# The third feed-forward part of a decoder: token lists per expert in place of all experts for every token

## The reference, cut to what matters

```python
shared = gelu(x @ ws1 + bs1) @ ws2 + bs2
aff = softmax(x @ Wr + br)                 # 31 experts
vals, idx = top_k(aff, 3)
gates = sum(one_hot(idx, 31) * vals[..., None], axis=-2)
for e in range(31):
    routed += gates[..., e] * (gelu(x @ We1[e] + Be1[e]) @ We2[e] + Be2[e])
x = layernorm(x + shared + routed + x)     # the part's own "+ x" and the residual
```

## Time and profile before

| | us |
|---|---|
| median of 3 runs (lowest, highest) | 2757.01 (2756.97, 2764.75) |
| the profiled execution, its own time | 2757.16 |
| its span, first to last instruction | 2755.4 |
| mean granted clock of TensorE | 0.846 |

### The profile page before, as it was taken

How to read it: one execution, slowest core, us unless ns; L and a number is a source line. 1 busy time by engine, 2 the same in 40 slices (tenths; PEclk the granted TensorE clock), 3 DMA queues, 4 the chain that set the end, 5 groups by cost and what they waited for, 6 DMA issues and landing times. The chain is left out here.

```text
span 2755.4 us, 44085 instructions
## 1 busy us (share of the span) xinstructions
PE 2173.7 (79%) x15402; PEld 1094.6 (40%) x15402; DVE 1629.0 (59%) x3578; ACT 1194.6 (43%) x2185; POOL 654.1 (24%) x845
## 2 busy tenths in 40 slices
PE   2699999975899996658999988629687773768888
PEld 1133355433233342634554444228422221335556
DVE  4588766577777732455676545235567772436666
ACT  0277756642267753223666675304232211433332
POOL 4211111134201110432121112044236673100000
PEclk9699999976589997777999998659888875779998
DMA  3300011100101010521111000038400001111111
GB/s 116 114 25 25 27 36 38 29 15 23 35 25 27 17 27 1 172 89 50 35 30 37 20 20 17 12 102 298 149 0 1 0 1 25 30 47 54 54 62 47
DMA packets 106846, 133.01 MB, mean 48 GB/s; under 512 B 26006, under 2 KB 90326, under 8 KB 105987
## 3 DMA queue, kind: packets, MB, share of 16 engines
q1 hardware_dynamic: 101556, 115.32, 14.0%
q0 software_dynamic: 3776, 7.79, 0.8%
q10 hardware_dynamic: 1296, 7.08, 0.7%
HBM read 70.65 MB, written 13.49 MB: 31 GB/s over the span
## 5 line engine op out<-in xcount | busy, mean ns | idle before, releaser
L1326 ACT ACTIVATE probs<-psE 128x512 f32<-128x512 f32 (+2 forms) x1248 | 698.0, 584 | 405.7 <-PE psE L1165 229.4
L1450 DVE TENSOR_REDUCE maxima<-psM 128x2 f32<-128x1024 f32 (+4 forms) x640 | 678.9, 1082 | 312.7 <-PE psM L1142 142.7
L1165 PE MATMUL psE<-q_stack,k_stack 53*128 53x512 bf16 (+3 forms) x1152 | 372.1, 361 | 36.6 <-ACT probs L1326 26.3
L1142 PE MATMUL psM<-k_stack,q_stack 51*128 51x512 bf16 (+3 forms) x1280 | 358.9, 352 | 32.2 <-DVE maxima L1450 13.9
L1601 POOL TENSOR_SCALAR pool_t<-mean_var 128x4 f32<-128x4 f32 x60 | 15.0, 250 | 935.7 <-DVE mean_var L1387 931.0
L2299 DVE SCALAR_TENSOR_TENSOR hres<-psM,gates,hres 128x128 f32<-128x128 f32 x512 | 144.2, 345 | 81.8 <-PE psM L2233 81.0
L1165 PEld LDWEIGHTS psE<-q_stack,k_stack 53*128 53x128 bf16 x1152 | 98.2, 94 | 229.2 <-ACT probs L1326 144.8
L1142 PEld LDWEIGHTS psM<-k_stack,q_stack 51*128 51x128 bf16 x1280 | 101.5, 96 | 196.2 <-issue 105.6
L1077 PE MATMUL psM<-masks_bf,ident_bf 64*128 64x128 bf16 (+2 forms) x832 | 148.3, 260 | 16.7 <-DMA k_stack<-k_parts 15.8
L2233 PEld LDWEIGHTS psM<-values,probs 128*128 128x128 f32 x1024 | 136.5, 195 | 59.4 <-issue 58.9
L1185 PE MATMUL psB<-probs,values 128*32 128x256 f32 (+3 forms) x1712 | 154.3, 432 | 2.4 <-ACT probs L1326 1.0
(11 more groups left out here) (411 smaller groups left out, 3614.4 us busy)
## 6 DMA issues: line engine op xcount, KB each, us to landing
q_stack<-q_parts SPq DMA_DIRECT2D x432, 64.0 KB
values<-experts_dram SPq DMA_DIRECT2D x40, 514.0 KB, 4.7
values<-experts_dram SPq DMA_DIRECT2D x32, 512.0 KB, 3.2
k_stack<-k_parts SPq DMA_DIRECT2D x192, 64.0 KB
hid<-experts_dram SPq DMA_DIRECT2D x15, 514.0 KB, 4.4
work<-experts_dram SPq DMA_DIRECT2D x15, 514.0 KB, 4.7
pack<-pack_dram SPq DMA_DIRECT2D x1, 4647.0 KB
work<-sorted SPq DMA_DIRECT2D x70, 65.0 KB, 3.7
```

The source lines that it names most:

```text
L1142: out, len(heads), keys, lo, max_mask(c, t), lambda i, to, start, stop: nc.tensor.matmul(to, q_stack[lo:lo + R_MAX, job.a % Q_SLOTS, pair_ ...
L1165: lambda h, to, start, stop: nc.tensor.matmul(to, ks[lo:lo + R_END, pairs[h], k * P:k * P + c.kn], q_stack[lo:lo + R_END, job.a % Q_SLOTS, ...
L1326: nc.scalar.activation(probs[0:c.kn, m % 2, heads[0]:heads[-1] + 1, q0:S], psE[0:c.kn, n % 2, 0:len(heads) * (S - q0)].rearrange("p (h q) ...
L1450: nc.vector.tensor_reduce(top, psM[:, at:at + len(banks), 0:per * keys].rearrange("p b (h k) -> p b h k", h=per), AX_X, ALU.max, negate=Tr ...
```

## The change

Part 3 now runs in `routed_experts` with n_exp = 31, top = 3, one block of 128 hidden features (`ft=1`), gelu in place of relu, and `shared=True`. `moe_stage`, `route` and `choose` are gone. NT is 16 * 3 + 30 = 78 tiles. The shared expert is computed for all tokens ahead of the tile loop: four up products of 512 tokens, four gelus, and its down product added in the bank of the experts' second biases. The output is stored from SP.

```diff
-        moe_stage(3, E3, E3 - 1, K3, 1, ACT.Gelu, "experts3", 4, residuals=2,
-                  store=lambda u: io["out"].rearrange("b (t p) d -> p b t d", p=P)[:, u:u + 1])
+        routed_experts(3, E3 - 1, K3, "experts3", ft=1, shared=True)
```

A third sorted buffer of (48 + 30) * 128 rows is added, and its clearing with it, in the first segment on ACT's queue:

```diff
-                       for li, n_exp, top in ((1, E1, K1), (2, E2, K2))]
-        CLEARS = 5
+                       for li, n_exp, top in ((1, E1, K1), (2, E2, K2), (3, E3 - 1, K3))]
+        CLEARS = 10
```

The counting on PE changes for all three parts. It was one accumulation with a 17th block of columns for the totals; now the totals are 16 products of their own into another bank:

```diff
-                    out = psB[:, 0:(G + 1) * n_exp]
-                    nc.tensor.matmul(out, earlier_bf[:, 0, :], picked_bf[:, 0:(G + 1) * n_exp], start=True, stop=False)
+                    out = psB[:, 0:G * n_exp]
+                    nc.tensor.matmul(out, earlier_bf[:, 0, :], picked_in(0, G), start=True, stop=False)
+                    for g in range(G - 1):
+                        nc.tensor.matmul(out[:, (g + 1) * n_exp:G * n_exp].rearrange("p (g e) -> p g e", e=n_exp),
+                                         earlier_bf[:, 1, :],
+                                         picked_in(g).unsqueeze(1).to_broadcast([P, G - 1 - g, n_exp]),
+                                         start=False, stop=g == G - 2)
                     for g in range(G):
-                        last = nc.tensor.matmul(
-                            out[:, (g + 1) * n_exp:(G + 1) * n_exp].rearrange("p (g e) -> p g e", e=n_exp),
...
+                        last = nc.tensor.matmul(psA[:, 0:n_exp], earlier_bf[:, 1, :], picked_in(g), start=g == 0,
+                                                stop=g == G - 1)
                     last.then_inc(ranked, 1)
```

For the shared expert (and the loop on one hidden block, where DVE has no share of the activation):

```diff
+                    if shared:
+                        pe.wait_ge(s_loaded, 16)
+                        for u in range(B):
+                            pe.wait_ge(g_taken, u + 1)
+                            nc.tensor.matmul(psM[:, u, :], w_shared[:, 0:P], xT[:, u, :], start=True, stop=True)\
+                                .then_inc(s_full, 1)
...
+                            if shared:
+                                last = nc.tensor.matmul(psE[:, u % 2, tokens], hid[:, u, tokens], w_shared[:, P:2 * P],
+                                                        start=False, stop=True)
...
-                        for f in range(FT1):
+                        for f in range(ft):
...
+                        for j in range(1, top):
+                            me.mark(nc.vector.tensor_tensor(hres[:, u], hres[:, u], back[u][j], ALU.add))
...
+                    if shared:
+                        for u in range(B):
+                            sp.wait_ge(x_done, u + 1)
+                            sp.dma_start(io["out"].rearrange("b (t p) d -> p b t d", p=P)[:, u], xt[:, u])\
+                                .then_inc(stored, 16)
```

More of the change, by code:

```diff
@@ L1713, in choose @@
[L1713 to L1742, removed]
@@ L1744, in routed_experts @@
-        def routed_experts(li, n_exp, top, weights, ahead=None):
+        def routed_experts(li, n_exp, top, weights, ft=FT1, ahead=None, shared=False):
             G = B * QT
@@ L1749, in routed_experts @@
             RW = D + 2
-            WIDE = 2 * FT1 * P + FT1
+            WIDE = 2 * ft * P + ft
             W_SLOTS, X_SLOTS, Y_SLOTS = 5, 7, 3
+            func = ACT.Gelu if shared else ACT.Relu
+            act_f = range(0, (ft + 1) // 2)
+            dve_f = range((ft + 1) // 2, ft)
             LAST_ROW = top * B * S
@@ L1790, in routed_experts @@
             peak_r, sum_r, first_r = (small(G) for _ in range(3))
-            gatesT = xT[0:32]
+            back = [[hres[:, u], xT[:, u].rearrange("p (t d) -> p t d", d=D),
+                     work[:, u].rearrange("p (t d) -> p t d", d=D)][0:top] for u in range(B)]
+            gated = n_exp + shared
             gate_all = gates[:].rearrange("p u t e -> p (u t) e")[:, :, 0:n_exp]
@@ L1909, in down_proj @@
                         out = (psA, psB)[i % 2][:, 0:D]
-                        for f in range(FT1):
-                            last = nc.tensor.matmul(out, hidden[:, i % 2, f, :], w[:, (FT1 + f) * P:(FT1 + f + 1) * P],
-                                                    start=f == 0, stop=f == FT1 - 1)
+                        for f in range(ft):
+                            last = nc.tensor.matmul(out, hidden[:, i % 2, f, :], w[:, (ft + f) * P:(ft + f + 1) * P],
+                                                    start=f == 0, stop=f == ft - 1)
                         last.then_inc(down, 1)
@@ L1925, in _ @@
                         down_proj(i)
-                    for u in range(B):
+                    for u in range(0 if shared else B):
                         pe.wait_ge(x_done, u + 1)
@@ L1939, in _ @@
                         act.wait_ge(g_full, u + 1)
-                        nc.scalar.copy(gatesT[0:n_exp, u, :], psM[0:n_exp, u, :]).then_inc(g_taken, 1)
+                        nc.scalar.copy(gatesT[0:gated, u, :], psM[0:gated, u, :]).then_inc(g_taken, 1)
+                    for u in range(B if shared else 0):
+                        act.wait_ge(s_full, u + 1)
+                        nc.scalar.activation(hid[:, u, :], psM[:, u, :], func, bias=w_shared[:, 2 * P:2 * P + 1])\
+                            .then_inc(s_taken, 1)
                     if ahead is not None:
@@ L1954, in _ @@
                         since(act, down, i - 1)
-                        for f in range(2):
+                        for f in act_f:
                             last = nc.scalar.activation(hidden[:, i % 2, f, :], psM[:, 2 * (i % 2), f * P:(f + 1) * P],
-                                                        ACT.Relu, bias=w_slot[i % W_SLOTS][:, 2 * FT1 * P + f:2 * FT1 * P + f + 1])
+                                                        func, bias=w_slot[i % W_SLOTS][:, 2 * ft * P + f:2 * ft * P + f + 1])
                         last.then_inc(act_h, 1)
-                    for u in range(B):
+                    for u in range(0 if shared else B):
                         act.wait_ge(x_full, u + 1)
@@ L2008, in _ @@
                         me.mark(nc.vector.tensor_tensor(both, picks[0], picks[1], ALU.add))
+                    for j in range(2, top):
+                        me.wait()
+                        me.mark(nc.vector.tensor_tensor(both, both, picks[j], ALU.add))
                     me.wait()
@@ L2090, in _ @@
                         dve.wait_ge(b_full, u + 1)
-                        nc.vector.tensor_tensor(flat(yt[:, u]), psE[:, u % 2, :], flat(xt[:, u]), ALU.add)\
-                            .then_inc(b_taken, 1)
+                        nc.vector.scalar_tensor_tensor(out=flat(yt[:, u]), in0=flat(xt[:, u]), scalar=2.0 if shared else 1.0,
+                                                       in1=psE[:, u % 2, :], op0=ALU.mult, op1=ALU.add).then_inc(b_taken, 1)
                     def finished(i):
@@ L2125, in _ @@
                         me.wait()
-                        if top == 2:
-                            me.mark(nc.vector.tensor_tensor(flat(hres[:, u]), flat(hres[:, u]), xT[:, u, :], ALU.add))
+                        for j in range(1, top):
+                            me.mark(nc.vector.tensor_tensor(hres[:, u], hres[:, u], back[u][j], ALU.add))
                             me.wait()
```

291 lines of the change are left out of this document (70 added, 221 removed).

## The result

The changed kernel takes 2728.0 us (median of four, 2723.1 to 2735.4) against 2757.0 of before in the same session; the ratio is 0.990, 95% interval 0.986 to 0.993. That is 29 us less where 39 were forecast: inside the range, but 10 us above the sum. The profiled execution took 2728.6 us, its span is 2726.6.

What follows compares the result with a forecast made beforehand. The prediction took PE to pace part 3's loop before the change and SP after it. Its terms summed as 2757.2 - 54.3 (part 3) + 4.4 (parts 1 and 2) + 11 (clearing) = 2718.3, forecast 2718 us, range 2704 to 2744.

Steps and rivals of the forecast that it cites:

- the sum: Whole kernel: all terms added, 2718 us, chance 0.62; first exp of the held-up group in the first segment at 144.
- The bound and the saving: Part 3: PE sets the old loop's pace, SP the new one's; 254.9 us against 309.2, a saving of 54.3.
- Head: Part 3, start to GpSimd's first scatter: 37.4 us, from part 2's 22.6 plus 14.8 for wider tables and added products.
- parts 1 and 2: Between picks and counts: 16 new products for the totals cost 2.2 us in each part, +4.4 together.
- Scatters: Part 3, first scatter to first row load: 48 scatters at 1.277 us each, 62.3 us in all.
- Everything else lies beside this: Part 3, scatters: VectorE's wide operations, shared expert and first weights are hidden, over some 30 us before the scatters are.
- Tile loop: Part 3, 78 tiles: SP's list sets a period of 1.57 us; 125.7 us with the ends.
- Tail: Part 3, after the tile loop: 29.5 us, from part 2's 22.8 plus a third load, third additions and the store.
- Clearing: First segment: five more clearing DMAs on ACT hold back the small load of the row maxima, +11 us.
- rival 2: First segment: clearing is interleaved with the small load, costing only ACT's 4.4 us; first exp at 137, time 2712; chance 0.13.
- Rivals 1 and 3: Part 3's loop: result buffers become the bound, 2732, chance 0.16; weight loads hold the row loads, 2765, chance 0.06.

Runs made afterwards that it cites:

- the spread one: Changed kernel with the five new clears issued one at a time, each behind a later output copy in the first segment; 2732.8 us, ratio 0.990.

## Why the prediction was right, and where its sum was off

**The bound and the saving: right.** Part 3 was PE's and is SP's; tiles, scatters and ends follow one another as laid out. The saving of part 3 is 38.8 of 54.3 forecast.

**Head: right to 2.4.** Of it 1.8 are the 16 products for the totals: 0.59 us for all, not 16 x 0.147. The 0.147 of the earlier trace rows is how long a weight load's record lasts, and I took it for the least distance of two loads. The 16 here overlap and follow each other 0.03 apart, and in the kernel before the products of 48, 32 and 16 columns already start 0.04 to 0.05 apart. That is also the mis-sized term of parts 1 and 2: forecast +2.2 each, measured +0.3 and +0.2 (first scatter 16.9 behind the start against 16.6, and 22.8 against 22.6).

**Scatters: the step that failed.** "Everything else lies beside this" took GpSimd and VectorE as independent. The stretch came out 7.8 us longer, and moving one input of the wide operations took 7.9 away. The sign was in the trace of before: one scatter of 1.28 in part 2 among 0.96s, beside a 752-column operation of two SBUF inputs. I averaged it into 1.277.

**Tile loop: the bound right, the period mis-sized.** 1.57 is the clean period of the loop and near its commonest, not its mean: one clean gap of the earlier trace rows stood for 72. At 1.68 they cost 8.1 more, of which 4.3 are the 18 long register loads; the ends are 0.8 off. The register load is what it rests on: with it gone the period is 1.40.

**Tail: 1.3 over.**

**Clearing: mis-sized, by a false reading.** I read the 7.0 us of the earlier trace rows as data in front of the small load, and took it as evidence against the even service of queues. It is SP's list of five issues, with 0.9 us behind the last, and it is 7 with either clearing. The clearing stretches it only in that SP's issues take about 1.3 us beside it in place of 0.65. The price until PE goes on is ACT's issues, 6.5 and not 4.4: the first two take 0.35 and 0.45 us, but from the fourth on each takes about 1.3. With SP's further slow issues the changed kernel is 9.6 behind the spread one soon after, which is near the 11, but by another mechanism. The first exp behind it comes at 141.4, between the 137 that I gave as rival 2's sign and the sum's 144. So rival 2's mechanism was right (interleaved), and its 4.4 too low. The rule of the Trainium skill that the prediction weighed, "DMA: Bandwidth & Descriptors" (section "Queues, rings and completion order"), agrees with these rows: the last small load, issued by 139.8, is there at 140.7, where the clears queued ahead of it take up to 18 us to land.

**The sum.** +15.5 in part 3 (-2.4, +7.8, +8.9, +1.3), -5.5 ahead of it: 10 us over 2718. The 9.9 us ahead of part 3 can't be split into causes. The changed kernel is 9.6 behind the kernel before at 500 us, 0.7 at 770, 9.3 at the start of part 1, 13.5 at that of part 2 and 9.9 at that of part 3, and in eleven profiles of the same code this last place scatters over 31 us. So that the stretch ahead of part 3 came out 5.5 below its forecast, and took back a third of part 3's error, is luck; without it the time would have been some 2733, still inside the range. Rivals 1 and 3 did not occur.

## What to carry to other kernels

Before calling two engines' work independent, look in the trace for one instruction of a group that is longer than its like, and at what stood beside it: one 1.28 among thirty 0.96s was an 8 us term. Take a period from its whole distribution, not from the cleanest gap. Where a queue engine paces a loop, look for a wait ahead of it in which part of its per-tile work can be paid; here it was 57 us long in the changed kernel, and using it gave the best one.

## What the runs showed that I had not expected

- A scatter of GpSimd that takes 0.96 us took up to 3.44 beside a 2.68 us VectorE operation with two SBUF inputs, and 0.96 with one of them in PSUM.
- SP's single instructions ran at 0.7 us each for stretches: some forty in three kernels, all with the row loads on ACT, and four to twelve in three with the row loads on SP, one of which has the changed kernel's own part 3. Not explained.
- The kernel with rows on ACT had waits for its result buffers, and yet with more of them its loop ran at 1.63 in place of 1.45 in the one profile taken, beside the slow instructions of SP.
- Beside the clearing data an issue of SP took about 1.3 us in place of 0.65, and the fourth and later clears in a row about 1.3 in place of 0.33.
- 9.6 us gained at 170 us were gone by 770 us in the same code, while the granted clock between 530 and 770 us was 0.71 in the kernel behind and 0.66 in the one ahead. On such a kernel a local gain below some 10 us shows in its stretch and may not show in the whole time.
